# Two chained cross-attention blocks on one core: the three neighbours' weighted values are added on VectorE before the transposes

## The reference

```python
q = split(rmsnorm(x_tokens, gamma_q) @ Wq.T)
kn = rmsnorm(ctx, gamma_kv)
k, v = split(kn @ Wk.T), split(kn @ Wv.T)
mask = (jnp.abs(ctx_pos - ctx_index_per_token[:, :, None]) <= 1)[:, None]
scores = jnp.einsum('bhqd,bhkd->bhqk', q, k) / math.sqrt(hd)
w = jnp.where(mask, jnp.square(jax.nn.relu(scores)), 0.0)
denom = jnp.maximum(w.sum(-1, keepdims=True), EPS_DEN)
out = jnp.einsum('bhqk,bhkd->bhqd', w / denom, v)
x = x_tokens + out.transpose(0, 2, 1, 3).reshape(B, T, D) @ Wo.T
```

```python
q, k, v = gelu(x @ Wq + bq), gelu(ctx @ Wk + bk), gelu(ctx @ Wv + bv)
w = softmax(q @ k.T)
x = layernorm((w @ v) @ Wf + bf + x) * ln_gamma + ln_beta
```

## Time and profile before

| what | value |
| --- | --- |
| median of 3 runs | 422.99 us (420.45 to 423.73) |
| profiled execution | 423.02 us |
| its span, from the first to the last instruction | 421.2 us |
| mean granted TensorE clock, as a share of full speed | 0.980 |
| busy: TensorE matmuls, weight loads | 384.7 us, 285.3 us |
| busy: VectorE, ScalarE, GpSimd | 300.5 us, 222.4 us, 143.7 us |

### The profile page before, as it was taken

The page is one execution under the profiler, slowest core; times in us unless marked ns, Lnnn a source line. Parts: engine busy times, 40 slices in busy tenths (PEclk is TensorE's granted clock), DMA queues, the critical chain, the costliest instruction groups (busy, mean ns, idle before and its releaser), DMA issues.

```text
span 421.2 us, 5934 instructions
## 1 busy us (share of the span) xinstructions
PE 384.7 (91%) x2256; PEld 285.3 (68%) x2256; DVE 300.5 (71%) x592; ACT 222.4 (53%) x369; POOL 143.7 (34%) x100
## 2 busy tenths in 40 slices
PE   4799798999999999999999999999999999998770
PEld 1258666686868686868686868686868777776550
DVE  0334459587979797878787887878787879697614
ACT  0754412356556564646464656565656474737441
POOL 0102202023535353535353535353535353415151
PEclk9999999999999999999999999999999999999985
DMA  8901985802121212121212112020202101010111
GB/s 238 321 38 43 219 213 158 193 2 75 51 75 52 75 51 75 51 75 51 75 53 72 54 55 71 30 95 15 93 26 82 42 0 52 0 51 0 50 51 50
DMA packets 20333, 32.35 MB, mean 77 GB/s; under 512 B 1489, under 2 KB 11729, under 8 KB 20305
## 3 DMA queue, kind: packets, MB, share of 16 engines
q1 hardware_dynamic: 18144, 24.11, 20.0%
q0 software_dynamic: 2160, 7.87, 5.3%
HBM read 17.29 MB, written 8.39 MB: 61 GB/s over the span
## 4 chain that ended last, share of the span: by engine, by line
PE 78%; ACT 6%; issue 4%; DVE 4%; DMA 3%; SPq 2%; POOL 2%; ACTq 0%; DVEq 0%; POOLq 0%
PE ps L373 11%; PE ps L375 10%; PE ps L374 10%; PE ps L411 9%; PE ps L509 7%; PE ps L465 7%; PE ps L386 7%; PE ps L392 5%; PE ps L441 4%; PE ps L324 4%; PE ps L516 3%; ACT bufs L629 2%; DMA cst<-consts 2%; PE ps L478 2%; DMA kv<-qkp 1%
## 5 line engine op out<-in xcount | busy, mean ns | idle before, releaser
L283 POOL TENSOR_TENSOR x_lo<-x_ring,x_hi 128x1024 fp32r<-128x1024 f32 x16 | 38.1, 2380 | 124.9 <-ACT x_hi L568 124.9
L585 ACT ACTIVATE bufs<-ps,nbias,rstd 128x256 f32<-128x256 f32 x64 | 32.4, 563 | 65.5 <-issue 55.5
L303 POOL TENSOR_TENSOR bufs<-bufs,lng_row 128x1024 f32<-128x1024 f32 x15 | 35.9, 2394 | 84.5 <-ACT bufs L585 84.5
L738 DVE TENSOR_TENSOR qkp<-ps,wn 128x1024 f32<-128x1024 f32 x48 | 57.3, 1221 | 5.9 <-PE ps L392 4.5
L697 DVE TENSOR_TENSOR qkp<-ps,bufs 128x1024 f32<-128x1024 f32 x48 | 57.1, 1218 | 5.2 <-PE ps L386 5.2
L411 PE MATMUL ps<-cst,qkp 128*128 128x128 f32 x384 | 44.8, 273 | 0.0
L411 PEld LDWEIGHTS ps<-cst,qkp 128*128 128x128 f32 x384 | 42.6, 143 | 0.1
L386 PE MATMUL ps<-onehot,kv 128*128 128x512 f32 x96 | 34.4, 440 | 4.7 <-DMA kv<-qkp 2.1
L509 PE MATMUL ps<-k1T,bufs 128*128 128x64 f32 x256 | 32.0, 278 | 5.4 <-ACT bufs L629 5.4
L305 POOL TENSOR_TENSOR bufs<-bufs,lnb_row 128x1024 f32<-128x1024 f32 x15 | 35.5, 2366 | 1.2
L509 PEld LDWEIGHTS ps<-k1T,bufs 128*128 128x128 f32 x256 | 29.8, 191 | 8.9 <-ACT bufs L629 8.9
(11 more groups left out here) (96 smaller groups left out, 820.8 us busy)
## 6 DMA issues: line engine op xcount, KB each, us to landing
x_ring<-xT SPq DMA_DIRECT2D x16, 512.0 KB, 3.6
out<-bufs POOLq DMA_DIRECT2D x15, 512.0 KB, 3.4
idx_ring<-idx SPq DMA_DIRECT2D x16, 256.0 KB, 4.2
kv<-qkp SPq DMA_DIRECT2D x8, 256.0 KB, 4.9
vfd<-bufs SPq DMA_DIRECT2D x4, 512.0 KB, 7.9
bufs<-ctxT SPq DMA_DIRECT2D x2, 512.0 KB, 6.5
qkp<-ctx SPq DMA_DIRECT2D x1, 1024.0 KB, 7.3
kv<-xp_hi SPq DMA_DIRECT2D x2, 256.0 KB, 4.1
```

What stands on the lines that cost most here:

```text
L283: G.tensor_tensor(x_lo[:, :, :], x_ring[:, f % RING, :, :], f32_view(x_hi[:, :, :]), ALU.subtract).then_inc(xl_ready, 2)
L303: G.tensor_tensor(zo, zn, lng_row[:, :].unsqueeze(1).broadcast_to([P, TT, D]), ALU.mult).then_inc(zg_ready, 1)
L738: V.tensor_tensor(att[:, s, :, :].rearrange("p j (h d) -> p (j h) d", d=HD), ps[:, bank0:bank0 + 2, :].rearrange("p a (h d) -> p (a h) d", ...
```

## The change

`attend` gets a destination. The products of neighbours 0 and 2 are written back over the PSUM banks from which they are read; the product of neighbour 1 goes to `att[:, 0]` in SBUF. A new function `add_shift` adds, on VectorE, first product 0 (PSUM) and product 1 (SBUF) into `att[:, 1]`, then product 2 (PSUM) and that sum into `att[:, 2]`, and counts up a new semaphore `sum_ready`. `turn` transposes only `att[:, 2]`, in 8 plain transposes, after both sums. Neighbour 2's values now go to banks 4 and 5, which are free after neighbour 1's product, instead of banks 6 and 7, which were free after neighbour 0's.

```diff
-            def turn(f, s):
+            def turn(f):
-                pe.wait_ge(att_ready, 3 * f + s + 1)
+                pe.wait_ge(sum_ready, 2 * f + 2)
                 for g in range(DC):
                     for j in range(TT):
-                        i = mm(ps[:, g, j * P:(j + 1) * P], att[:, s, j, g * P:(g + 1) * P], ident,
-                               is_transpose=True, start=(s == 0 and j == 0), stop=(s == SHIFTS - 1), skip_group_check=True)
-                    if s == SHIFTS - 1:
-                        i.then_inc(o_mm, 1)
+                        i = nc.tensor.transpose(ps[:, g, j * P:(j + 1) * P], att[:, 2, j, g * P:(g + 1) * P], ident)
+                    i.then_inc(o_mm, 1)
...
                 if f is not None:
-                    pe.wait_ge(att_ready, 3 * f + 1)
-                    picked_values(f, 2, 6)
+                    pe.wait_ge(att_ready, 3 * f + 2)
+                    picked_values(f, 2, 4)
...
-                    for s in range(SHIFTS):
-                        turn(f, s)
+                    turn(f)
...
+                def picked(bank0):
+                    return ps[:, bank0:bank0 + 2, :]
+
-                def attend(s, bank0):
+                def attend(s, bank0, dst):
                     dve.wait_ge(vg_mm, 3 * f + s + 1)
-                    V.tensor_tensor(att[:, s, :, :].rearrange("p j (h d) -> p (j h) d", d=HD),
-                                    ps[:, bank0:bank0 + 2, :].rearrange("p a (h d) -> p (a h) d", d=HD),
+                    V.tensor_tensor(dst.rearrange("p a (h d) -> p (a h) d", d=HD),
+                                    picked(bank0).rearrange("p a (h d) -> p (a h) d", d=HD),
                                     wn[:, s, :, :].rearrange("p j h -> p (j h)").unsqueeze(2).broadcast_to([P, TT * H, HD]),
                                     ALU.mult).then_inc(att_ready, 1)
+
+                def att_flat(i):
+                    return att[:, i, :, :].rearrange("p (a j) d -> p a (j d)", a=2)
+
+                def add_shift(s, bank0, dst):
+                    dve.wait_ge(att_ready, 3 * f + s + 1)
+                    if s == 2:
+                        dve.wait_ge(sum_ready, 2 * f + 1)
+                    V.tensor_tensor(att_flat(dst), picked(bank0), att_flat(dst - 1), ALU.add).then_inc(sum_ready, 1)
...
-                    attend(0, 6)
-                    attend(1, 4)
-                    attend(2, 6)
+                    attend(0, 6, picked(6))
+                    attend(1, 4, att_flat(0))
+                    add_shift(1, 6, 1)
+                    attend(2, 4, picked(4))
+                    add_shift(2, 4, 2)
```

More of the change, by code:

```diff
@@ L131, in xattn_pair @@
             "q0_mm", "q0_cp", "kg_mm", "qk_ready", "s_mm", "s_cp", "sT_mm", "w_ready"))
-        den_ready, dcl_ready, rden_ready, wn_ready, vg_mm, att_ready, o_mm, oh_ready, ol_ready = map(sem, (
-            "den_ready", "dcl_ready", "rden_ready", "wn_ready", "vg_mm", "att_ready", "o_mm", "oh_ready", "ol_ready"))
+        den_ready, dcl_ready, rden_ready, wn_ready, vg_mm, att_ready, sum_ready, o_mm, oh_ready, ol_ready = map(sem, (
+            "den_ready", "dcl_ready", "rden_ready", "wn_ready", "vg_mm", "att_ready", "sum_ready", "o_mm", "oh_ready", "ol_ready"))
         xp_mm, xp_ready, xph_ready, xpl_ready, q1_mm, q1_ready, sc_mm = map(sem, (
```

## The result

| | before | after |
| --- | --- | --- |
| median (range, runs) | 423.36 us (420.45 to 425.65, 4) | 457.25 us (456.46 to 458.46, 4) |
| ratio of after to before | | 1.081, 95% interval 1.074 to 1.088 |
| profiled execution, its span | 423.02 us, 421.2 us | 457.49 us, 455.7 us |
| mean granted TensorE clock | 0.980 | 0.948 |

What follows compares the result with a forecast made beforehand. Two chains, TensorE's and VectorE's, were taken to end each step nearly together, the change lengthening VectorE's. 423.0 + 30.9 (14 x 1.95 + 2.5 + 1.1) + 3.4 for clock falls = 457 us; range 449 to 473, forecast case 450 to 465.

Steps and rivals of the forecast that it cites:

- What bounds the kernel: End of a step: TensorE's chain and VectorE's, from first product to `o_lo` (8.88 us), end within 0.1 us of each other.
- The transposes taken away count for nothing: TensorE, end of a step: 16 fewer transposes save 1.75 us, which turn up as part of 2.6 us of new waiting.
- +1.95 us a step: Net lengthening of a step: +2.52 for the five passes, -0.09 and -0.37 for holes, -0.1 for overlaps at starts.
- The holes: VectorE's idle gaps of 0.09 us before the row maximum and 0.37 us before `o_lo`, both expected to close.
- The five passes: VectorE's three products and two additions: 3.68 + 2 x 1.22 + 2 x 0.04 = 6.20 us, ending 2.52 us later.
- A PSUM target costs nothing: VectorE's two products written over their own PSUM banks: no surcharge taken, upper end 2.2 us a step.
- Rival 2: VectorE's products over their own banks are slower, up to 1.09 us each: 492 us, or 475; chance 0.08.
- TensorE's new waits: End of a step: TensorE waits about 1.1 us for the second addition and 1.5 us for the softmax weights.
- The clock: TensorE's sparse stretch at a step's end lets the clock fall to half; two falls of 1.7 us taken, 3.4 us.
- this case: The forecast case: whole kernel at 457 us with none to five clock falls, range 450 to 465, chance 0.78.
- Rival 1: Not slower: VectorE's five passes fit under TensorE, taking no longer than 4.14 us; 417 us, chance 0.03.
- Rival 3: TensorE's clock falls in each of 14 steps: 454 + 14 x 1.7 = 478 us; chance 0.09.

Runs made afterwards that it cites:

- experiment 5: Kernel before with a second one-hot buffer and the one-hot matrix built ahead of the weights, no other edit; 423.09 us, ratio 0.999.
- experiment 2: Kernel before with only neighbour 2's product transposed (8 transposes instead of 24) and nothing added on VectorE; 417.48 us, ratio 0.985.
- experiment 1: Kernel before, its 24 transposes kept, with two VectorE additions of 1024 elements whose results nobody uses; 449.45 us, ratio 1.060.
- experiment 3: Changed kernel with the residual's eight transposes done three times instead of once, filling TensorE's holes; 449.04 us, ratio 1.060.
- experiment 8: Changed kernel with the products of neighbours 0 and 2 in a spare SBUF buffer, both additions reading SBUF alone; 476.78 us, ratio 1.127.

## Why the prediction was right, point by point

**What bounds the kernel.** Right, and shown from both sides. Shortening VectorE's chain alone gives nothing (experiment 5), shortening TensorE's alone gives 0.48 us a step (experiment 2) where the prediction had 0.4. The two chains tie in where they end, not in length: the hole of 0.37 us before `o_lo` was a wait for TensorE's transposes, so TensorE's chain was the longer one by about that much.

**The transposes taken away count for nothing.** Right, and more than that: experiment 1 keeps them and has the same step at full clock, and is 8 us faster because the clock holds.

**+1.95 us a step.** The mechanism is right, the size was not: it is 1.49 us (10.37 against 8.88). The holes closed as forecast. Two terms of the sum were mis-sized.
- The five passes were put at 6.20 us from the first start to the last end. They take 6.02 (134.35 to 140.37). I had read the old row "3.68 us for three" as three passes back to back. Where nothing holds them, starts are 1.14 us apart after the change (134.35, 135.49), not 1.23. In the old row the second start is 1.14 us after the first too (212.30, 213.44), but the third product starts at 214.76, 0.10 us after the second ended, right behind TensorE's pick. A merged row of the timeline hides such short waits.
- From the end of the second addition to the row maximum it was put at 0.91 us, from the old one-hot matrix (1.07 us for two parts). It takes 0.70. In the kernel before, the one-hot matrix started while GpSimd was still adding beta; afterwards, it starts later than that:

```profile
L684 DVE TENSOR_SCALAR onehot<-idx_ring,cst x48: 473/478/682, 45.4 to 369.4; 128x512 fp32r<-128x512 int32 x48
```

That was the single line of the one-hot matrix before (ns, minimum/median/maximum), and GpSimd's timeline before beside it is:

```profile
213.92 2.37 POOL L305 TENSOR_TENSOR bufs<-bufs,lnb_row 128x1024 f32<-128x1024 f32 x1
```

Here the matrix started at 215.90, and GpSimd ended at 216.29. The trace has 13 such parts that start while GpSimd adds beta, and they take 670 to 682 ns; the 35 others take 473 to 482. After the change none starts beside it, and none takes over 483 ns. That GpSimd is the cause is thus argued from the trace and from experiment 8's like case; it was not tried by itself.

The rest, some 0.05 us, is in smaller overlaps.

**A PSUM target costs nothing.** Right: 1.228 us at the median (1.222 to 1.233), against 1.224. Rival 2 is out.

**TensorE's new waits.** Forecast 1.1 and 1.5 us, measured 1.27 and 1.13, the second shorter because the weights come earlier than in the sum.

**The clock.** The mechanism is right (experiment 3), the number too small: two falls of 1.7 us were taken. In batches 1 to 14, four of 1.55 us lengthened a step, and one of 1.0 us that of batch 14 (22.74 against 21.7 us in experiments 1 and 3). One more lies in the step of batch 0 (clock 0.85, 4.2 us longer than before, where 2.5 had been forecast for the additions). From batch 15's first product to the end of the span it is 39.4 us instead of 36.9, 1.4 us more than forecast; there too the trace has a fall that the kernel before does not have, from 432.2 to 435.6. Falls whose place is covered by TensorE's own waits cost nothing.

**Why 457 came out.** At full clock batches 1 to 14 cost some 20.5 us (12 x 1.5, and 1.3 and 1.2 for batches 1 and 14, read from experiment 3) where 27.3 were forecast, 7 too few. The falls in them cost 7.2 where 3.4 were taken, the one in batch 0 another 1.7, and the end 1.4: 7 more. The measured 34.5 us of span stand against 34.3 in the sum. The agreement to a microsecond is luck; what the method was worth is its range of 450 to 465 for this case.

**Rivals.** Rival 1 (not slower) is out; but its price was right: 417 us is what 8 transposes without additions give. Rival 3 (a fall in each step) is out.

## What to carry to other kernels

Before moving work from the busiest engine to a less busy one, find the stretch in which the other engine itself has no holes, and look at the chain through it with both lengths side by side: an engine at 71% can be the one that sets the time. Work that must be added to such a chain is free only if something of like size leaves it for the engine's real idle time, as the one-hot matrix did, and if no more is added than the cover (here one addition, until the scores end). And count what the relieved engine does with its free time: on TensorE, holes can cost clock at the place that hurts.

## What the hardware showed that I had not expected

- A VectorE addition with both operands in SBUF took 2.67 us instead of 1.22 when it started during GpSimd's addition, and ended 1.08 us after it, 14 times in one kernel. With one operand in PSUM, the same addition took 1.22 to 1.23 us throughout. Over the kernel this was 20 us.
- A part of the one-hot matrix took 670 to 682 ns in place of 478 each time that it started during GpSimd's addition (13 of 48 parts, kernel before).
- Sixteen useless transposes a step made the changed kernel 8 us faster, by keeping the granted clock at 1.00 in the steps of batches 1 to 14.
- A fall of the clock of the same 3.4 us cost 0 or 1.55 us, depending on whether TensorE was waiting for VectorE at the time.
